# A fused attention and mixture-of-experts layer: the router's choice of groups by eight-largest and match-replace, and its steps placed on other tiles

## The chip, the cores and the metric

The kernel runs on one core of one Trainium2 chip. The number is the device time of one execution in microseconds (us). Durations inside come from one profiled execution.

## The reference

The layer takes x of shape (8, 512, 128), normalises it, puts it through 16-head attention with a residual and a second layer norm, adds that to x, normalises again and applies a mixture of 64 experts and one shared expert. What matters here is the router:

```python
scores = sigmoid(x @ router_w.T)                      # 64 experts
sfc = scores + e_bias
group_scores = top_k(sfc.reshape(T, 8, 8), 2)[0].sum(-1)   # 8 groups of 8
_, gidx = top_k(group_scores, 4)                      # best 4 groups
masked = where(expert in one of those groups, sfc, 0)
_, topk_idx = top_k(masked, 8)                        # best 8 experts
w = scores at topk_idx;  w = w / (w.sum(-1) + 1e-20) * 2.5
coef = w scattered to (T, 64)
h = silu(x @ Wg) * (x @ Wu) * coef ;  moe_out = h @ Wd (summed over experts)
```

Each of the eight sequences (512 tokens, 4 row tiles of 128) is one "block" of the expert part.

## The kernel before

The program has two parts. The first is attention over 64 pairs (sequence, two heads). The second is the expert part: eight blocks, numbered 0 to 7, of 33 tiles each: tile 0 is the shared expert, tiles 1 to 32 hold two experts each. All arithmetic on TensorE (PE) is done in split fp16, three matmuls for a product. Every engine has its own instruction stream, written out in order, and semaphores tie the streams together.

In iteration k of a block (`run_block`), PE issues `gate_up(k + 4)` (3 + 3 matmuls with 512 columns for a tile's gate and up products), then `down(k)` (3 matmuls that add tile k into the output). For one tile, ScalarE (ACT) applies silu (L693), VectorE (DVE) multiplies the up product with the coefficient row (L1006) and that with the gate (L1014, the tile is then `hid`), ACT makes the high half (L698), GpSimd (POOL) the low half (L535), and `down` takes both. Gate and up products lie in rings of three banks: `gate_up(t)` waits until `hid` of tile t-3 is there. So in iteration k PE waits for DVE's tile k + 1.

While block n runs, the routing of block n + 1 is computed in steps `route(m, r, k)`, k from 1 to 30. Four tables, `DVE_N`, `POOL_N`, `ACT_N` and `PE_N`, say behind which tile (on POOL, ahead of which tile) each engine does which step. Blocks 1 to 7 are routed this way; block 0 is routed during the last attention pairs, by the tables ending in `_0`. The steps are:

- 1 to 8: the second and third norm. POOL does the powers (L467, L469, steps 3 and 8), adds beta to x (L488, step 2), multiplies by gamma (L473) and adds x (L477); ACT scales rows (L610 in steps 4 and 5, L617 in 9 and 10). Step 7 on DVE reads what L477 wrote.
- 8 on PE (L1095): four transposes of the normed block, waiting for `xf_done` of ACT's step 10. ACT's 11 (L623) and DVE's 12 (L864) split the result, PE's 11 (12 matmuls with 64 columns) makes the logits.
- 14: ACT's sigmoid (L626), which reloads its function table before and after, and POOL's bias (L483).
- 16 to 19 on DVE: the two largest of each group and their sum, `gsum`. 20 to 22: the best four groups, by comparing all pairs of groups (L898 to L909). 23: the mask (L913). 24 and 25: the eight best experts (L918, L922). 26 to 28: normalised coefficients; L935 ends step 28 and raises `coef`.
- 27 on PE (L1110): four transposes of the coefficients. PE waits for `coef` in front of the `down` that comes before them. ACT's 30 (L630) copies them out, SyncE writes them to HBM and reads them back as rows broadcast over 64 partitions, two per tile, for L1006.

At a block's end, ACT copies the sum of the block before (L703, behind tile 3), PE turns it (L1251) and DVE adds it (L1019). `down` of the new block's tile 0 waits for that copy.

```python
                    if k == 27 and not last:
                        pe.wait_ge(coef, n + 2)
                    down(n, r, k)
```

`DVE_TAIL`, `PE_TAIL` and their like carry the last attention pieces in block 0 and are not changed. The functions and their callers:

Of the kernel before, what the change touches and what calls it, by code (L numbers as in the profile page):

```python
# [18 lines left out]
P = 128  # L19
# [11 lines left out]
QT = S // P  # L31
# [17 lines left out]
ROUTE_0 = 56  # L49


DVE_0 = {0: (1,), 1: (2,), 2: (3,), 9: (7,), 10: (8,), 15: (12,), 21: (16,), 22: (17,), 23: (18, 19), 24: (20, 21),
         25: (22, 23), 26: (24,), 27: (25,), 28: (26,), 29: (27,), 30: (28,)}
POOL_0 = {0: (1,), 2: (2,), 3: (3,), 7: (6,), 10: (8,), 20: (14,)}
ACT_0 = {5: (4,), 6: (5,), 12: (9,), 13: (10,), 15: (11,), 19: (14,), 31: (30,)}
PE_0 = {15: (8,), 19: (11,), 31: (27,)}


DVE_N = {1: (1,), 2: (2,), 3: (3,), 8: (7,), 9: (8,), 15: (12,), 19: (16,), 20: (17,), 21: (18, 19), 22: (20, 21),
         23: (22, 23), 24: (24,), 25: (25,), 26: (26,), 27: (27,), 28: (28,)}  # L60
POOL_N = {3: (3,), 5: (2,), 6: (6,), 9: (8,), 17: (14,)}
ACT_N = {5: (4,), 6: (5,), 11: (9,), 12: (10,), 14: (11,), 17: (14,), 30: (30,)}
PE_N = {11: (8,), 14: (11,), 27: (27,)}


PE_TAIL_UP = {2: ((64, 0),), 3: ((64, 1),), 4: ((64, 2), (64, 3))}
# [5 lines left out]
def layer(nc, x, Wq, bq, Wk, bk, Wv, bv, Wo, bo, gamma, beta, router_w, e_bias,  # L72
          Wg, Wu, Wd, SWg, SWu, SWd, out):
    with ExitStack() as ctx:  # L74
        def sem(name):
            return ctx.enter_context(nc.semaphore(name))
# [71 lines left out]
        ya = tiles4(take(S))  # L148
        bn, mean_var = tiles4(take(QT * 6)), tiles4(take(QT * 2))
        veps, rstd, total, share, nmean, shift = (take(QT) for _ in range(6))  # L150
        tri = take(G * G)
        assert top[0] <= xT_hi_at + dead
        top[0] = xT_lo_at
        xf = tiles4(take(S))
# [98 lines left out]
        route_step = sem("route_step")  # L253
        coef_out = sem("coef_out")
        coef_in = [sem(f"coef_in{i}") for i in range(4)]
        tri_done = sem("tri_done")
        g_ps = sem("g_ps")
        u_ps = sem("u_ps")
        silu_done = sem("silu_done")
# [170 lines left out]
        def _(pool):  # L430
# [23 lines left out]

            def route(m, r, k):

                if k == 1 and isinstance(m, int) and m == 0:

                    pool.wait_ge(scores_t, 8 * ROUTE_0)
                    pool.memset(tri, 1.0).then_inc(tri_done, 1)  # L460
                    pool.wait_ge(tri_done, 1)
                    pool.affine_select(out=tri.rearrange("p (g h) -> p g h", g=G), in_=tri.rearrange("p (g h) -> p g h", g=G),
                                       compare_op=ALU.is_gt, fill=0.0, base=0, pattern=[[1, G], [-1, G]],
                                       channel_multiplier=0).then_inc(tri_done, 1)
                if k in (3, 8):
                    pool.wait_ge(c_var, m * 2 + (1 if k == 3 else 2))
                    pool.tensor_tensor(rstd, veps, half_pow, ALU.pow).then_inc(rstd_pow, 1)  # L467
                    pool.wait_ge(rstd_pow, m * 2 + (1 if k == 3 else 2))
                    pool.tensor_tensor(shift, nmean, rstd, ALU.mult).then_inc(rstd_done, 1)  # L469
                if k == 6:  # L470

                    pool.wait_ge(scaled, m + 1)
                    pool.tensor_tensor(ya, ya, gamma_b.unsqueeze(1).broadcast_to([P, QT, D]), ALU.mult).then_inc(gained, 1)  # L473
                    wait(pool, out_sent, (m - 1) * 16)
# [250 lines left out]
        def _(dve):  # L725
# [95 lines left out]
            def route(m, r, k):  # L821
# [65 lines left out]
                if k == 19:  # L887
                    settled()
                    then(nc.vector.tensor_tensor(sec1, mid1, lo1, ALU.max))
                    own(nc.vector.tensor_tensor(gsum, hi1, sec1, ALU.add))  # L890

                mine = gsum.rearrange("p (t g) -> p t g", t=QT).unsqueeze(3).broadcast_to([P, QT, G, G])
                other = gsum.rearrange("p (t g) -> p t g", t=QT).unsqueeze(2).broadcast_to([P, QT, G, G])
                pairs3, pairs4 = (w.rearrange("p (t g h) -> p t g h", t=QT, g=G) for w in (work3, work4))
                taken, masked = (w.rearrange("p (t e) -> p t e", t=QT) for w in (work3, work4))
                if k == 20:
                    settled()
                    own(nc.vector.tensor_tensor(pairs4, other, mine, ALU.is_gt))  # L898
                    own(nc.vector.tensor_tensor(pairs3, other, mine, ALU.is_ge))
                if k == 21:  # L900
                    settled()
                    if isinstance(m, int) and m == 0:
                        dve.wait_ge(tri_done, 2)
                    then(nc.vector.tensor_tensor(taken, taken, all_tiles(tri), ALU.mult))
                    own(nc.vector.tensor_tensor(work3, work3, work4, ALU.max))
                if k == 22:
                    settled()
                    then(nc.vector.tensor_reduce(rank, work3.rearrange("p (n h) -> p n h", h=G), AX.X, ALU.add))
                    own(nc.vector.tensor_scalar(rank, rank, float(TOPG) - 0.5, None, ALU.is_lt))  # L909

                if k == 23:
                    settled()
# [129 lines left out]
        def _(pe):  # L1042
# [211 lines left out]
            def run_block(n, r, last):  # L1254
                for k in range(1, TILES if last else TILES + 1):
                    if not (last and k + 4 >= TILES):
                        gate_up(n, r, k + 4)
                    if k == 27 and not last:
                        pe.wait_ge(coef, n + 2)
                    down(n, r, k)  # L1260
                    if isinstance(n, int) and n == 0:
                        tail(run, PE_TAIL.get(k, ()))
                    if not last:
                        for part in PE_N.get(k, ()):
                            route(n + 1, 1 - r, part)
                transpose_sum(n, last)
# [3 lines left out]
            for k in range(5):  # L1270
# [54 lines left out]
```

## Time and profile before

| | |
|---|---|
| three runs, median (lowest to highest) | 1362.97 us (1359.21 to 1363.02) |
| the profiled execution | 1363.27 us, of which its span 1361.5 us |
| mean granted TensorE clock | 0.988 |
| PE busy, share of the span | 1295.1 us, 95% |
| VectorE busy | 1069.7 us, 79% |
| GpSimd busy | 1047.5 us, 77% |
| ScalarE busy | 870.9 us, 64% |
| expert part, end of the first block to the end | from about 868.8 to 1361.5 us |

Engine names in rows: PE is TensorE's matmuls, DVE is VectorE, ACT is ScalarE, POOL is GpSimd. L1044 is the helper through which nearly all matmuls pass. The timeline merges neighbouring instructions of one line (xN); the bracket is the idle time ahead of the row and what ended it.

### The profile page before, as it was taken

The page shows a single profiled execution, that of the slowest core. Times are in us where ns is not written, and L with a number is a line of the kernel's source. Part 1 is how long each engine was busy: PE and PEld are TensorE (multiplying, and loading weights), DVE is VectorE, ACT ScalarE, POOL GpSimd, SP SyncE. Part 2 cuts the span into 40 slices and gives each one's busy share as a digit, 9 for nine tenths or more (in the row PEclk, how much of TensorE's full clock was granted, in tenths as well). Part 3 has the DMA queues.
Part 4 walks back from the last instruction along what each step waited for, and adds up shares of the span by engine and source line. Part 5 has one row for each costly group of instructions (what it writes and reads, how often), then busy time and mean ns, then how long its engine had stood idle before and what let it go on. Part 6 is the DMA issues. An engine that isn't in the chain of part 4 may idle for free. (4 is left out here: it accounts for less than half of the span.)

```text
span 1361.5 us, 36458 instructions
## 1 busy us (share of the span) xinstructions
PE 1295.1 (95%) x12729; PEld 755.1 (55%) x12729; DVE 1069.7 (79%) x1898; ACT 870.9 (64%) x1588; POOL 1047.5 (77%) x1705
## 2 busy tenths in 40 slices
PE   3999999999999999999999899999999998999998
PEld 1576666666666666666666544444444343444443
DVE  6788888887777777777787878778877878787875
ACT  4677766666666666666666556566656575656554
POOL 2888888888888888888898866767667675767665
PEclk9899999999999999999999999999999999999999
DMA  7333333333333333333333043434343444434342
GB/s 188 78 83 78 82 78 73 86 76 81 74 78 79 82 75 79 78 81 75 81 81 79 6 128 117 135 117 144 117 132 123 121 134 121 131 116 148 100 157 91
DMA packets 126428, 135.60 MB, mean 100 GB/s; under 512 B 36112, under 2 KB 83536, under 8 KB 126288
## 3 DMA queue, kind: packets, MB, share of 16 engines
q1 hardware_dynamic: 126288, 133.71, 35.5%
q8 instruction: 91, 1.49, 0.5%
q14 instruction: 49, 0.40, 0.1%
HBM read 80.16 MB, written 3.15 MB: 61 GB/s over the span
## 5 line engine op out<-in xcount | busy, mean ns | idle before, releaser
L1044 PE MATMUL bank<-arena 128*128 128x65 f16 (+4 forms) x12344 | 1265.2, 264 | 51.3 <-DVE arena L1014 14.4
L1044 PEld LDWEIGHTS bank<-arena 128*128 128x128 f16 (+2 forms) x12344 | 709.8, 98 | 573.0 <-DVE arena L1014 37.8
L499 POOL TENSOR_TENSOR arena<-arena 128x256 f16<-128x256 f32 x1024 | 596.4, 614 | 102.5 <-ACT arena L654 101.6
L535 POOL TENSOR_TENSOR arena<-arena 128x256 f16<-128x256 f32 x528 | 344.6, 679 | 153.4 <-ACT arena L698 151.3
L950 DVE TENSOR_REDUCE arena<-bank 128x2 f32<-128x1024 f32 x256 | 311.9, 1219 | 54.2 <-PE bank L1044 50.3
L654 ACT ACTIVATE arena<-bank 128x512 f32<-128x512 f32 x512 | 276.6, 595 | 63.1 <-PE bank L1044 63.0
L698 ACT ACTIVATE arena<-arena 128x512 f16<-128x512 f32 x264 | 164.5, 623 | 156.3 <-DVE arena L1014 154.0
L1014 DVE TENSOR_TENSOR arena<-arena,bank 128x512 f32<-128x512 f32 x264 | 181.7, 688 | 61.5 <-ACT bank L693 38.0
L1006 DVE TENSOR_TENSOR arena<-arena,bank 128x512 f32<-128x512 f32 x256 | 174.9, 683 | 43.8 <-PE bank L1044 25.7
L693 ACT ACTIVATE bank<-bank 128x512 f32<-128x512 f32 x264 | 153.2, 581 | 46.7 <-PE bank L1044 46.3
L643 ACT ACTIVATE arena<-bank,arena 128x512 f16<-128x512 f32 x128 | 87.9, 687 | 143.1 <-PE bank L1044 143.1
L981 DVE SCALAR_TENSOR_TENSOR arena<-bank,arena 128x512 f16<-128x512 f32 x128 | 95.5, 746 | 17.6 <-ACT arena L643 14.6
L658 ACT ACTIVATE arena<-bank 2x1024 f16<-2x1024 f32 x64 | 64.9, 1014 | 22.0 <-PE bank L1044 21.8
L987 DVE TENSOR_TENSOR arena<-bank,arena 128x512 f16<-128x512 f32 x64 | 44.3, 691 | 40.9 <-ACT arena L675 40.9
L970 DVE TENSOR_TENSOR arena<-bank,arena 128x256 f32<-128x256 f32 x128 | 54.3, 424 | 4.4
L968 DVE RECIPROCAL arena<-bank 128x4 f32<-128x4 f32 x128 | 23.2, 182 | 35.5 <-PE bank L1044 35.4
L681 ACT ACTIVATE arena<-bank 128x512 f16<-128x512 f32 x64 | 37.7, 589 | 9.6 <-PE bank L1225 9.6
L959 DVE TENSOR_TENSOR arena<-bank,arena 128x512 f32 (+1 forms) x64 | 43.6, 681 | 0.0
L976 DVE TENSOR_TENSOR arena<-bank,arena 128x512 f16<-128x512 f32 x64 | 43.6, 681 | 0.0
L1225 PE MATMUL bank<-arena 128*128 128x128 f32 x256 | 39.3, 277 | 2.8 <-DVE arena L959 2.8
L1225 PEld LDWEIGHTS bank<-arena 128*128 128x128 f32 x256 | 32.4, 144 | 15.5 <-DVE arena L959 3.4
L675 ACT ACTIVATE arena<-bank 128x512 f16<-128x512 f32 x64 | 38.4, 600 | 2.4 <-PE bank L1044 0.9
(103 smaller groups left out, 415.9 us busy)
## 6 DMA issues: line engine op xcount, KB each, us to landing
arena<-coef_rows SPq DMA_DIRECT2D x512, 128.0 KB, 2.9
arena<-arena SPq DMA_DIRECT2D x384, 128.0 KB, 2.4
arena<-in_L_attn_x SPq DMA_DIRECT2D x9, 256.0 KB, 3.8
arena<-in_L_ffn_Wg SPq DMA_DIRECT2D x32, 64.0 KB, 2.2
arena<-in_L_ffn_Wu SPq DMA_DIRECT2D x32, 64.0 KB, 2.1
arena<-in_L_ffn_Wd SPq DMA_DIRECT2D x32, 64.0 KB, 2.1
out<-arena SPq DMA_DIRECT2D x8, 256.0 KB, 2.9
coef_rows<-arena SPq DMA_DIRECT2D x8, 128.0 KB, 2.2
```

What stands on the lines that cost most here:

```text
L499: last = pool.tensor_tensor(num_lo[:, u % 2, s, h, q], num[:, u % 2, s, h, q], num_hi[:, u % 2, s, h, q, 1], ALU.subtract)
L535: last = pool.tensor_tensor(hid_lo[:, r, at], hid[:, r, at], hid_hi[:, r, at], ALU.subtract)
L643: nc.scalar.activation(flat[:, (u + 3) % 2, (ZQH, ZKH)[which], :], proj_bank(t, which), ACT.Identity, bias=bias[:, n:n + 1]).then_inc(qk_h ...
L654: nc.scalar.activation(num[:, u % 2, s, h, :], ps_st[ST_BANK[2 * s + h]], ACT.Exp).then_inc(exp_done, 1)
L693: nc.scalar.activation(ps_gate[r % 3], ps_gate[r % 3], ACT.Silu).then_inc(silu_done, 1)
L698: nc.scalar.activation(hid_hi[:, r, :], hid[:, r, :], ACT.Copy).then_inc(hid_hi_done, 1)
L950: nc.vector.tensor_reduce(rmax[:, up % 2, q, :], max_bank(pair, q).rearrange("p (h k) -> p h k", h=2), AX.X, ALU.max).then_inc(max_done, 1)
L981: nc.vector.scalar_tensor_tensor(out=flat[:, (u + 3) % 2, (ZQL, ZKL)[s], :], in0=proj_bank(t, s), scalar=(bq8, bk_c)[s][:, n:n + 1], in1=f ...
L1006: nc.vector.tensor_tensor(prod[:, i % 2, :], coef_b[:, j % 4, :], ps_up[i % 3], ALU.mult).then_inc(prod_done, 1)
L1014: nc.vector.tensor_tensor(hid[:, i % 6, :], prod[:, i % 2, :], ps_gate[i % 3], ALU.mult).then_inc(hid_done, 1)
L1044: return nc.tensor.matmul(out_, lhsT, rhs, start=start, stop=stop, skip_group_check=True)
L1225: last = nc.tensor.transpose(ps_turn[:, k * P:(k + 1) * P], ctxn[:, u % 2, k, :], ident)
```

## The change

Three things change.

1. The best four groups are found as the experts are: `max` gives each row's eight group sums in falling order, a `memset` overwrites the last four of them with 3e38, `match_replace` puts -3e38 where one of the values that are left occurs, and a compare makes the mask. The pair comparisons, their triangle mask `tri` (POOL's step 1 of block 0) and step 22 go. The sums are over 4 row tiles, so `max` and `match_replace` are issued four times each, on 8 elements.
2. The tables place the steps on other tiles.
3. POOL's multiplication by gamma (L473) becomes step 5 of its own, ahead of tile 6; the addition of x (L477) stays step 6 and comes ahead of tile 7.

```diff
-DVE_N = {1: (1,), 2: (2,), 3: (3,), 8: (7,), 9: (8,), 15: (12,), 19: (16,), 20: (17,), 21: (18, 19), 22: (20, 21),
-         23: (22, 23), 24: (24,), 25: (25,), 26: (26,), 27: (27,), 28: (28,)}
-POOL_N = {3: (3,), 5: (2,), 6: (6,), 9: (8,), 17: (14,)}
-ACT_N = {5: (4,), 6: (5,), 11: (9,), 12: (10,), 14: (11,), 17: (14,), 30: (30,)}
-PE_N = {11: (8,), 14: (11,), 27: (27,)}
+DVE_N = {1: (1,), 2: (2,), 3: (3,), 9: (7,), 10: (8,), 15: (12,), 18: (16,), 19: (17,), 20: (18, 19), 21: (20,),
+         22: (21,), 23: (23,), 24: (24,), 25: (25,), 26: (26,), 27: (27, 28)}
+POOL_N = {3: (3,), 4: (2,), 6: (5,), 7: (6,), 10: (8,), 17: (14,)}
+ACT_N = {5: (4,), 6: (5,), 12: (9,), 13: (10,), 15: (11,), 17: (14,), 29: (30,)}
+PE_N = {10: (8,), 12: (11,), 24: (27,)}
...
                 if k == 19:
                     settled()
                     then(nc.vector.tensor_tensor(sec1, mid1, lo1, ALU.max))
-                    own(nc.vector.tensor_tensor(gsum, hi1, sec1, ALU.add))
+                    then(nc.vector.tensor_tensor(gsum, hi1, sec1, ALU.add))
...
+                groups, left = (w.rearrange("p (t g) -> p t g", t=QT) for w in (gsum, rank))
+                first = work2[:, 0:QT * G].rearrange("p (t g) -> p t g", t=QT)
                 if k == 20:
+                    for t in range(QT):
+                        own(nc.vector.max(first[:, t, :], groups[:, t, :]))
                     settled()
-                    own(nc.vector.tensor_tensor(pairs4, other, mine, ALU.is_gt))
-                    own(nc.vector.tensor_tensor(pairs3, other, mine, ALU.is_ge))
+                    own(nc.vector.memset(first[:, :, TOPG:], 3.0e38))
+                    settled()
                 if k == 21:
+                    for t in range(QT):
+                        own(nc.vector.match_replace(left[:, t, :], first[:, t, :], groups[:, t, :], -3.0e38))
                     settled()
-                    if isinstance(m, int) and m == 0:
-                        dve.wait_ge(tri_done, 2)
-                    then(nc.vector.tensor_tensor(taken, taken, all_tiles(tri), ALU.mult))
-                    own(nc.vector.tensor_tensor(work3, work3, work4, ALU.max))
-                if k == 22:
-                    settled()
-                    then(nc.vector.tensor_reduce(rank, work3.rearrange("p (n h) -> p n h", h=G), AX.X, ALU.add))
-                    own(nc.vector.tensor_scalar(rank, rank, float(TOPG) - 0.5, None, ALU.is_lt))
+                    own(nc.vector.tensor_scalar(rank, rank, -2.0e38, None, ALU.is_lt))
...
-                    if k == 27 and not last:
+                    if k == 24 and not last:
                         pe.wait_ge(coef, n + 2)
                     down(n, r, k)
```

The tables of block 0 change less: on DVE, behind the same slots, step 20 alone and then 21 and 23; on POOL `tri` goes, and the new steps 5 and 6 stand side by side as before.

**PE, a block with routing.** These are the matmuls of block 0's stream from the end of the attention pieces on; 9 matmuls with 512 columns are one iteration, L1095 (after: L1083) the norm's transposes, 128x64 the logits, L1110 (after: L1098) the coefficients' transposes, L1251 (after: L1239) the turned sum. Before:

```order
L1044 MATMUL bank<-arena 128x512 x54
L1095 MATMUL bank<-arena 128x128 x4
L1044 MATMUL bank<-arena 128x512 x27
L1044 MATMUL bank<-arena 128x64 x12
L1044 MATMUL bank<-arena 128x512 x117
L1110 MATMUL bank<-arena 64x128 x4
L1044 MATMUL bank<-arena 128x512 x54
L1251 MATMUL bank<-arena 128x128 x4
```

After:

```order
L1032 MATMUL bank<-arena 128x512 x45
L1083 MATMUL bank<-arena 128x128 x4
L1032 MATMUL bank<-arena 128x512 x18
L1032 MATMUL bank<-arena 128x64 x12
L1032 MATMUL bank<-arena 128x512 x108
L1098 MATMUL bank<-arena 64x128 x4
L1032 MATMUL bank<-arena 128x512 x81
L1239 MATMUL bank<-arena 128x128 x4
```

The norm's transposes moved up by one iteration, the logits by two, the coefficients' transposes by three.

**DVE, steps 20 to 24.** L1006 and L1014 (after: L994 and L1002) are the two multiplications of a tile; REGISTER_ALU rows prepare waits. Before, tiles 22 and 23:

```order
L1014 TENSOR_TENSOR arena<-arena,bank 128x512
L831 REGISTER_ALU
L898 TENSOR_TENSOR arena<-arena 128x256
L899 TENSOR_TENSOR arena<-arena 128x256
L831 REGISTER_ALU
L904 TENSOR_TENSOR arena<-arena 128x256
L831 REGISTER_ALU
L905 TENSOR_TENSOR arena<-arena 128x256
L1002 REGISTER_ALU
L1006 TENSOR_TENSOR arena<-arena,bank 128x512
L1014 TENSOR_TENSOR arena<-arena,bank 128x512
```

After, tiles 21 and 22:

```order
L1002 TENSOR_TENSOR arena<-arena,bank 128x512
L889 MAX arena<-arena 128x8 x4
L823 REGISTER_ALU
L891 MEMSET arena 128x4x4
L823 REGISTER_ALU
L990 REGISTER_ALU
L994 TENSOR_TENSOR arena<-arena,bank 128x512
L1002 TENSOR_TENSOR arena<-arena,bank 128x512
L895 MATCH_REPLACE arena<-arena 128x8 x4
L823 REGISTER_ALU
L897 TENSOR_SCALAR arena<-arena 128x32
L990 REGISTER_ALU
```

Four instructions on 256 elements (and two more behind the next tile) became ten on at most 32, spread over two tiles, one tile earlier.

## Rows read from the trace of the kernel before

Blocks are counted from 0. Iteration 12 of block 3 starts at 1036.38 us.

**Rows 1.** PE timeline, block 3: start us, us, engine, line, tiles, count [idle before].

```profile
1036.38 19.94 PE L1044 MATMUL bank<-arena 128*128 128x512 f16 x102
...
1057.44 2.12 PE L1044 MATMUL bank<-arena 128*128 128x512 f16 x9 [1.13 <-DVE arena L1014]
...
1071.37 11.17 PE L1044 MATMUL bank<-arena 128*128 128x512 f16 x51
...
1083.48 0.81 PE L1044 MATMUL bank<-arena 128*128 128x512 f16 x3 [0.93 <-ACT arena L703]
...
1084.12 0.60 PE L1251 MATMUL bank<-arena 128*128 128x128 f32 x4
```

**Rows 2.** PE timeline, last block: one stretch of 29 iterations without a wait.

```profile
1298.39 56.66 PE L1044 MATMUL bank<-arena 128*128 128x512 f16 x261
```

**Rows 3.** DVE timeline, block 3, tiles 18 to 28 with the routing of block 4.

```profile
1045.07 0.69 DVE L1014 TENSOR_TENSOR arena<-arena,bank 128x512 f32<-128x512 f32 x1 [2.62 <-ACT bank L693]
...
1053.99 0.42 DVE L898 TENSOR_TENSOR arena<-arena 128x256 f32<-128x256 f32 x1
...
1055.93 0.67 DVE L1006 TENSOR_TENSOR arena<-arena,bank 128x512 f32<-128x512 f32 x1
...
1057.30 0.41 DVE L908 TENSOR_REDUCE arena<-arena 128x32 f32<-128x256 f32 x1
...
1057.97 0.43 DVE L913 TENSOR_TENSOR arena<-arena 128x256 f32<-128x256 f32 x1
...
1059.97 0.60 DVE L918 MAX8 arena<-arena 128x8 f32<-128x64 f32 x4
...
1060.78 0.69 DVE L1006 TENSOR_TENSOR arena<-arena,bank 128x512 f32<-128x512 f32 x1 [0.21 <-DVE arena L918]
...
1062.16 0.08 DVE L922 MATCH_VALUE_LOAD arena<-arena 128x8 f32 x1
...
1062.36 0.08 DVE L922 MATCH_VALUE_LOAD arena<-arena 128x8 f32 x1
...
1068.84 0.42 DVE L935 TENSOR_TENSOR arena<-arena 128x256 f32<-128x256 f32 x1
```

**Rows 4.** ACT timeline, block 3, around the sigmoid.

```profile
1041.04 1.28 ACT L626 ACT_TABLE_LOAD   x1
...
1042.76 0.38 ACT L626 ACTIVATE arena<-bank 128x256 f32<-128x256 f32 x1 [0.43 <-PE bank L1044]
...
1044.45 0.58 ACT L693 ACTIVATE bank<-bank 128x512 f32<-128x512 f32 x1
```

**Rows 5.** DVE timeline, block 4's first tile with a coefficient.

```profile
1078.18 0.69 DVE L1006 TENSOR_TENSOR arena<-arena,bank 128x512 f32<-128x512 f32 x1 [1.80 <-DMA arena<-coef_rows]
```

**Rows 6.** PE timeline, six block periods: first and last of seven sums.

```profile
868.76 0.91 PE L1251 MATMUL bank<-arena 128*128 128x128 f32 x4
...
1297.95 0.60 PE L1251 MATMUL bank<-arena 128*128 128x128 f32 x4
```

**Rows 7.** PE timeline, blocks 4 to 5: a boundary with a longer wait.

```profile
1155.65 1.44 PE L1044 MATMUL bank<-arena 128*128 128x512 f16 x3 [2.11 <-ACT arena L703]
...
1156.88 1.06 PE L1251 MATMUL bank<-arena 128*128 128x128 f32 x4
...
1157.74 11.82 PE L1044 MATMUL bank<-arena 128*128 128x512 f16 x51
```

**Rows 8.** Windows: length, PE PEld DVE ACT POOL busy (count), PEclk, DMA, GB/s.

```profile
1157.00:1159.00 2.00, 2.00 (x8) 1.11 (x7) 0.99 (x6) 0.56 (x1) 0.00 (x0) 0.50 0.37 131
```

**Rows 9.** PE timeline, block 4: its sixth tile, and the norm's transposes.

```profile
1096.59 10.53 PE L1044 MATMUL bank<-arena 128*128 128x512 f16 x48 [0.86 <-POOL arena L535]
...
1106.96 0.60 PE L1095 MATMUL bank<-arena 128*128 128x128 f32 x4
```

**Rows 10.** ACT timeline, block 4: the second half of the norm's scaling.

```profile
1102.82 0.86 ACT L617 ACTIVATE arena<-arena 128x128 f32<-128x128 f32 x2
```

**Rows 11.** POOL timeline, attention part, after `tri` was made (686.7 to 687.5 us).

```profile
689.93 2.32 POOL L499 TENSOR_TENSOR arena<-arena 128x256 f16<-128x256 f32 x4 [0.16 <-ACT arena L654]
```

More of the change, by code:

```diff
@@ L49 @@
 ROUTE_0 = 56
-DVE_0 = {0: (1,), 1: (2,), 2: (3,), 9: (7,), 10: (8,), 15: (12,), 21: (16,), 22: (17,), 23: (18, 19), 24: (20, 21),
-         25: (22, 23), 26: (24,), 27: (25,), 28: (26,), 29: (27,), 30: (28,)}
-POOL_0 = {0: (1,), 2: (2,), 3: (3,), 7: (6,), 10: (8,), 20: (14,)}
+DVE_0 = {0: (1,), 1: (2,), 2: (3,), 9: (7,), 10: (8,), 15: (12,), 21: (16,), 22: (17,), 23: (18, 19), 24: (20,),
+         25: (21, 23), 26: (24,), 27: (25,), 28: (26,), 29: (27,), 30: (28,)}
+POOL_0 = {2: (2,), 3: (3,), 7: (5, 6), 10: (8,), 20: (14,)}
 ACT_0 = {5: (4,), 6: (5,), 12: (9,), 13: (10,), 15: (11,), 19: (14,), 31: (30,)}
 PE_0 = {15: (8,), 19: (11,), 31: (27,)}
-DVE_N = {1: (1,), 2: (2,), 3: (3,), 8: (7,), 9: (8,), 15: (12,), 19: (16,), 20: (17,), 21: (18, 19), 22: (20, 21),
-         23: (22, 23), 24: (24,), 25: (25,), 26: (26,), 27: (27,), 28: (28,)}
-POOL_N = {3: (3,), 5: (2,), 6: (6,), 9: (8,), 17: (14,)}
-ACT_N = {5: (4,), 6: (5,), 11: (9,), 12: (10,), 14: (11,), 17: (14,), 30: (30,)}
-PE_N = {11: (8,), 14: (11,), 27: (27,)}
+DVE_N = {1: (1,), 2: (2,), 3: (3,), 9: (7,), 10: (8,), 15: (12,), 18: (16,), 19: (17,), 20: (18, 19), 21: (20,),
[3 more added lines that the diff above has]
+PE_N = {10: (8,), 12: (11,), 24: (27,)}
 PE_TAIL_UP = {2: ((64, 0),), 3: ((64, 1),), 4: ((64, 2), (64, 3))}
@@ L150, in layer @@
         veps, rstd, total, share, nmean, shift = (take(QT) for _ in range(6))
-        tri = take(G * G)
         assert top[0] <= xT_hi_at + dead
@@ L255, in layer @@
         coef_in = [sem(f"coef_in{i}") for i in range(4)]
-        tri_done = sem("tri_done")
         g_ps = sem("g_ps")
@@ L455, in route @@
             def route(m, r, k):
[L457 to L464, printed above, removed]
                 if k in (3, 8):
@@ L469, in route @@
                     pool.tensor_tensor(shift, nmean, rstd, ALU.mult).then_inc(rstd_done, 1)
-                if k == 6:
+                if k == 5:
                     pool.wait_ge(scaled, m + 1)
                     pool.tensor_tensor(ya, ya, gamma_b.unsqueeze(1).broadcast_to([P, QT, D]), ALU.mult).then_inc(gained, 1)
+                if k == 6:
                     wait(pool, out_sent, (m - 1) * 16)
@@ L889, in route @@
                     then(nc.vector.tensor_tensor(sec1, mid1, lo1, ALU.max))
-                    own(nc.vector.tensor_tensor(gsum, hi1, sec1, ALU.add))
-                mine = gsum.rearrange("p (t g) -> p t g", t=QT).unsqueeze(3).broadcast_to([P, QT, G, G])
-                other = gsum.rearrange("p (t g) -> p t g", t=QT).unsqueeze(2).broadcast_to([P, QT, G, G])
-                pairs3, pairs4 = (w.rearrange("p (t g h) -> p t g h", t=QT, g=G) for w in (work3, work4))
+                    then(nc.vector.tensor_tensor(gsum, hi1, sec1, ALU.add))
                 taken, masked = (w.rearrange("p (t e) -> p t e", t=QT) for w in (work3, work4))
+                groups, left = (w.rearrange("p (t g) -> p t g", t=QT) for w in (gsum, rank))
+                first = work2[:, 0:QT * G].rearrange("p (t g) -> p t g", t=QT)
                 if k == 20:
+                    for t in range(QT):
+                        own(nc.vector.max(first[:, t, :], groups[:, t, :]))
                     settled()
-                    own(nc.vector.tensor_tensor(pairs4, other, mine, ALU.is_gt))
-                    own(nc.vector.tensor_tensor(pairs3, other, mine, ALU.is_ge))
+                    own(nc.vector.memset(first[:, :, TOPG:], 3.0e38))
+                    settled()
                 if k == 21:
+                    for t in range(QT):
+                        own(nc.vector.match_replace(left[:, t, :], first[:, t, :], groups[:, t, :], -3.0e38))
                     settled()
-                    if isinstance(m, int) and m == 0:
-                        dve.wait_ge(tri_done, 2)
-                    then(nc.vector.tensor_tensor(taken, taken, all_tiles(tri), ALU.mult))
-                    own(nc.vector.tensor_tensor(work3, work3, work4, ALU.max))
-                if k == 22:
-                    settled()
-                    then(nc.vector.tensor_reduce(rank, work3.rearrange("p (n h) -> p n h", h=G), AX.X, ALU.add))
-                    own(nc.vector.tensor_scalar(rank, rank, float(TOPG) - 0.5, None, ALU.is_lt))
+                    own(nc.vector.tensor_scalar(rank, rank, -2.0e38, None, ALU.is_lt))
                 if k == 23:
@@ L1300 @@
 ROUTE_COUNT = {1: 1, 2: QT, 3: QT + 1, 7: QT, 8: QT + 1, 16: 2, 17: 4, 18: 3, 19: 2,
-               20: 2, 21: 2, 22: 2, 23: 1, 24: QT, 25: QT, 26: 2, 27: 3, 28: 0}
+               20: QT + 1, 21: QT + 1, 23: 1, 24: QT, 25: QT, 26: 2, 27: 3, 28: 0}
 ROUTE_AT = {k: sum(c for j, c in ROUTE_COUNT.items() if j < k) for k in ROUTE_COUNT}
```

## The prediction

> **What bounds the kernel now.** I read first the timeline of PE over the expert part. Without a wait PE needs 56.66 us for 261 matmuls, 29 iterations, 1.95 us each [rows 2]. That is the floor, so only what makes PE wait, or slows its clock, counts. A routed block costs 33 x 1.95 = 64.4 us, three sets of transposes at 0.44 (1298.39 - 1297.95 [rows 2, 6]), and the logits' 0.4 (the stretch of x102 lasts 19.94, ten iterations 19.5 [rows 1]): 66.1 us. The six periods between the first and last sum of [rows 6] take (1297.95 - 868.76)/6 = 71.5. So 5.4 us of each block are waits and low clock.
>
> Then I looked at where. There are three places. (a) Near iteration 22 PE waits for DVE's `hid`, first 1.13 us [rows 1], then in smaller pieces, about 3 in all. DVE has no idle time there: from tile 18's L1014 at 1045.07 to the end of L935 at 1069.26 it runs for 24.19 us [rows 3], because a tile costs it only 1.37 (L1006 at 1055.93 to L908 at 1057.30), less than PE's 1.95, but routing steps lie between. The lag that PE forgives is large: `hid` of a tile may be about 3 us late. (b) At the boundary `down` of tile 0 waits for L703: 0.93 us [rows 1], 2.11 in another block [rows 7]. What is late is the coefficient rows: DVE waits 1.80 for them at the first tile [rows 5], and L703 stands behind that tile's successors on ACT. (c) In iteration 6 `down` waits 0.86 for POOL [rows 9].
>
> A wait has a second price. After the 2.11 us wait the granted clock is 0.50, the 1.2 GHz level [rows 8], and the same work takes longer than after the wait of 0.93: 1.44 against 0.81, 1.06 against 0.60, 11.82 against 11.17 [rows 7, 1], together 1.7 us. After the 1.13 and 0.93 waits nothing of it is seen.
>
> **The DVE steps.** Steps 20 to 22 take 1055.93 - 1053.99 = 1.94 and 1057.97 - 1057.30 = 0.67, together 2.61 us [rows 3]. The new ones aren't in the trace. Nearest rows: four `max` on 64 elements take 0.60, and 0.81 until the next tile starts; a value load and its match-replace follow each other every 0.20 (1062.16 to 1062.36) [rows 3]. On 8 elements I take 0.07 for each `max` and 0.14 for each pair, since narrower rows take less, plus some 0.2 to 0.25 each for the memset and the compare with the waits around them: 0.63 + 0.77 = 1.4. From above, at the 64-wide price: 0.81 + 0.25 and 0.80 + 0.45 = 2.3; from below 1.0. The saving is 1.2 us a block (0.3 to 1.6). Two further `settled` (step 19, and between 27 and 28) cost about 0.15.
>
> The Trainium skill (VectorE: DVE Perf Modes, the section on the TRN2 errata) speaks against this edit: an fp32 two-input operation takes (N + 151)/0.96 ns, so small ones pay nearly the whole fixed part each time, 166 ns for 8 elements. By that alone steps 20 and 21 would cost about 2.0 us, the saving would be 0.6, and the sum below would end 4 us higher. The pitch of the `max` and match-replace rows is shorter than the durations that this rule gives, so the trace does not bear it out for a run of such instructions without a wait between them.
>
> **The new order.** The important move is PE's. `pe.wait_ge(coef)` stood in iteration 27 and now stands in iteration 24, ahead of `down(24)`, while DVE raises `coef` behind tile 27 instead of 28. In a PE stream that does not wait, `gate_up(31)` has been issued by iteration 27, DVE is long past tile 28, and no wait for `coef` shows in [rows 1]. In iteration 24 it has only just issued `gate_up(28)`. Working it out in block 3:
>
> - PE: iteration 12 starts at 1036.38 before [rows 1], and by the terms under POOL below at nearly the same time after. Twelve iterations, the logits, and the 1.3 of a `gate_up`: 1036.4 + 23.4 + 0.4 + 1.3 = 1061.5, and some 0.15 for `hid` of tile 25, 1061.65. (The waits of (a) are gone up to there: steps 16 on start a tile earlier and 20 to 22 are shorter, so the lag of DVE passes 3 us only at tile 25.)
> - ACT: the sigmoid now waits for nothing. Before, it waited 0.43 for the logits, and ACT came to its table load (1041.04) late as well, since it had been held by the wait for the transposes. Table load, sigmoid and second load still take 1.28 + 0.4 + 1.28 ahead of tile 18's silu [rows 4]. I get 0.9 us earlier (0.43 + 0.45), so tile 18's L1014 at 1044.2.
> - DVE: from there without idle time, as before: 24.19, less one tile (1.37), less 1.2, plus 0.15: 21.75. `coef` comes at 1065.95.
>
> PE waits 1065.95 - 1061.65 = 4.3 us. Behind the wait stand `down(24)`, the transposes and `gate_up(29)`, so DVE runs dry too. Bounds: with 0.3 us more of a gain on ACT and the cheapest new steps 3.6; without any ACT gain and with the dearest 6.1.
>
> After it the clock. A wait of 2.11 was followed by the low level, waits of 1.13 and less were not, so one of 4.3 should be; I take the 1.7 us of above. Bounds: 0.9, if half of the low stretch falls into the wait, 2.6, if it lasts half as long again.
>
> **What the boundary gives back.** Relative to iteration 28 the coefficients leave about 4 us earlier. The 1.80 that they were late [rows 5] is covered, L703 runs when `down(32)` is done, and both the 0.93 and the 2.11 with its low clock go. I take zero for the boundary.
>
> **POOL.** L477 comes one L535 pair (1.3 us) later, so `down(6)` no longer waits [rows 9]; `down(7)` may for 0.2. But the norm is a chain: L477, step 7, step 8, L467, ACT's steps 9 and 10, PE's transposes. It now ends some 1.1 us later, while the transposes stand one iteration (1.95) earlier and the 0.86 that held PE up ahead of them is mostly gone. Before, ACT finished at 1102.82 + 0.86 = 1103.68 and the transposes began at 1106.96, 3.3 us later [rows 9, 10]. 3.3 - 1.1 - 1.95 - 0.8 = -0.6: PE waits 0.6 for `xf_done`. Bounds 0 to 1.2. Logits earlier by two iterations: ACT's step 11 stands at tile 15, its input is there, and the split is ready about 0.4 us before PE wants it: no wait.
>
> **Attention part.** Without `tri` POOL has two short operations less; 2.4 us later it idled 0.16 anyway [rows 11], so nothing is won. DVE's saving there is followed by waits on PE and ACT. I take 0, plus or minus 1.
>
> **The sum.** A block after: 66.1 + 0.2 (POOL) + 0.6 (norm) + 0.15 + 4.3 (`coef`) + 1.7 (clock) = 73.05, against 71.5: +1.55, six times +9.1 (from the unrounded mean). Block 0 with the routing of block 1 has the same new wait and loses a boundary wait of 2 us: +1. Total +10: 1363.3 + 10.1 = 1373.4 us. The profiled execution lies 0.3 above the median, so the same number stands against the runs.
>
> **Rivals.**
> 1. As worked out, 1373.4 (1367 to 1381 by the bounds): 0.57.
> 2. The new wait is there, but the clock stays at 2.4 GHz or the low stretch falls into the wait: seven times 1.7 less, 1361.5, no change. Against it: [rows 7, 8]. 0.12.
> 3. Faster. If DVE is much less behind at tile 27, the boundary's gain decides. The floor of 66.1 with 0.8 for POOL and norm leaves 4.6 for `coef` and clock before the block is as long as now; a wait of 1.5 without loss of clock gives 68.4, 3.1 less a block, 1342. It needs DVE 2.8 us earlier than I find. For it: with no lag at all the wait would be about 1. Against: the unbroken 24 us of DVE [rows 3]. 0.16.
> 4. Much slower: new steps at the dearest, ACT without its gain, and the longer low clock, 6.1 + 2.6 in place of 6.0: 2.7 a block more, about 1392. 0.05.
> 5. The new wait is real but costs only what (a) and (b) cost now, because DVE, not PE, sets the block: 1360 to 1366. 0.05.
> 6. The new steps cost the 2.3 us of the 64-wide rows, 0.9 more: `coef` and PE come later by that in seven blocks, 1373.4 + 6.3 = 1379.7. 0.05. This is what a fixed cost per instruction would do here; the rule of the Trainium skill named above (VectorE: DVE Perf Modes, TRN2 errata) is of that kind.
>
> **How the numbers follow.** A difference of 0.3% (4 us) is about what can be told. Slower: the first case but for 0.02 that falls short, the fourth and the sixth: 0.65. Same: the second, most of the fifth, those 0.02: 0.18. Faster: the third and the rest: 0.17. Range: up to 1382 it leaves out the fourth case; down to 1361 it takes in the second, and leaves out the third.
>
> **What would show it.** PE's timeline has one wait of 4 to 5 us for DVE (the coefficient product, L923 in the new file) ahead of three matmuls and the four transposes, in each of seven blocks, with a granted clock of 0.5 behind it; no wait for L703's counterpart; DVE idle behind the transposes; a wait of about 0.6 at the norm's transposes; none for POOL above 0.3. The four `max` on 8 elements take near 0.37. I am wrong if the `coef` wait is under 3 us, or if the clock stays high after it.

## The result, and the profile after

The changed kernel takes 1388.93 us (median of 4 runs, 1387.83 to 1389.89) against 1361.47 us (median of 4) for the kernel before on the same chip: ratio 1.021, 95% interval [1.0196, 1.0224]. It is slower, as forecast, but by 27 us and not by 10, and outside the range of 1361 to 1382. The profiled execution has a span of 1388.0 us.

PE's timeline in block 3 after (start us, us, engine, line, tiles, count, [idle before]), which answers to [rows 1]:

```profile
1023.24 19.64 PE L1032 MATMUL bank<-arena 128*128 128x512 f16 x90
1043.68 0.66 PE L1083 MATMUL bank<-arena 128*128 128x128 f32 x4 [0.79 <-ACT arena L609]
1044.17 27.78 PE L1032 MATMUL bank<-arena 128*128 128x512 f16 x135
1076.64 1.46 PE L1032 MATMUL bank<-arena 128*128 128x512 f16 x3 [4.69 <-DVE arena L923]
1077.90 1.06 PE L1098 MATMUL bank<-arena 128*64 128x128 f32 x4
1078.75 18.21 PE L1032 MATMUL bank<-arena 128*128 128x512 f16 x81
1096.80 0.60 PE L1239 MATMUL bank<-arena 128*128 128x128 f32 x4
```

The forecast wait is the fourth row: PE idles 4.69 us for DVE's L923 (the step that raises `coef`) ahead of `down(24)`, and the next row is the four transposes. The second row is the wait for `xf_done`, 0.79. The three matmuls behind the long wait take 1.46 us, the transposes 1.06, where [rows 1] has 0.81 and 0.60: the low clock. The stretch before the sum shows no wait for L695 (L703 before), and there is none for POOL in iteration 6.

Two rows each from other places on PE: the periods' first and last sum, which answer to [rows 6], and a wait for `hid` and one at a boundary, which answer to [rows 1, 7]:

```profile
870.64 0.60 PE L1239 MATMUL bank<-arena 128*128 128x128 f32 x4
...
1140.65 5.66 PE L1032 MATMUL bank<-arena 128*128 128x512 f16 x24 [0.45 <-DVE arena L1002]
...
1173.02 0.81 PE L1032 MATMUL bank<-arena 128*128 128x512 f16 x3 [2.20 <-ACT arena L695]
...
1324.42 0.60 PE L1239 MATMUL bank<-arena 128*128 128x128 f32 x4
```

Six periods take (1324.42 - 870.64)/6 = 75.6 us, against 71.5 before. At the boundary behind block 4, PE still waits 2.20 us for L695. I had put that at zero.

The granted clock behind a wait for `coef`, by windows (us, PE, PEld, DVE, ACT, POOL busy, PEclk, DMA share, GB/s), which answers to [rows 8]:

```profile
999.00:1001.00 2.00, 1.17 (x3) 0.46 (x4) 1.91 (x3) 0.00 (x0) 1.30 (x2) 0.50 0.36 94
1001.00:1003.00 2.00, 2.00 (x8) 1.14 (x7) 0.15 (x1) 0.00 (x0) 0.00 (x0) 0.50 0.49 120
1003.00:1005.00 2.00, 2.00 (x6) 0.71 (x5) 0.17 (x1) 1.54 (x3) 0.35 (x1) 0.55 0.03 11
1005.00:1007.00 2.00, 2.00 (x11) 0.88 (x9) 1.42 (x3) 0.91 (x3) 0.95 (x2) 1.00 0.32 74
```

The wait ends at 999.83. The clock stands at 0.50, the 1.2 GHz level, from then to beyond 1003, and is back at 1.00 in the last row.

DVE in block 3, which answers to [rows 3], with two rows of block 3's start:

```profile
1013.51 0.69 DVE L1002 TENSOR_TENSOR arena<-arena,bank 128x512 f32<-128x512 f32 x1 [0.19 <-DVE arena L998]
1016.86 0.69 DVE L994 TENSOR_TENSOR arena<-arena,bank 128x512 f32<-128x512 f32 x1 [2.67 <-PE bank L1032]
...
1053.99 0.69 DVE L1002 TENSOR_TENSOR arena<-arena,bank 128x512 f32<-128x512 f32 x1 [1.46 <-ACT bank L685]
...
1061.86 0.36 DVE L889 MAX8 arena<-arena 128x8 f32<-128x8 f32 x4
1062.30 0.07 DVE L891 MEMSET arena<- 128x16 f32 x1
1062.56 0.69 DVE L994 TENSOR_TENSOR arena<-arena,bank 128x512 f32<-128x512 f32 x1 [0.19 <-DVE arena L891]
...
1063.94 0.08 DVE L895 MATCH_VALUE_LOAD arena<-arena 128x8 f32 x1
...
1064.60 0.18 DVE L897 TENSOR_SCALAR arena<-arena 128x32 f32<-128x32 f32 x1
1064.77 0.69 DVE L994 TENSOR_TENSOR arena<-arena,bank 128x512 f32<-128x512 f32 x1
...
1066.15 0.42 DVE L901 TENSOR_TENSOR arena<-arena 128x256 f32<-128x256 f32 x1
...
1075.68 0.91 DVE L923 TENSOR_TENSOR arena<-arena 128x256 f32<-128x256 f32 x1
1076.51 0.67 DVE L994 TENSOR_TENSOR arena<-arena,bank 128x512 f32<-128x512 f32 x1
```

The first two rows are tile 0 and tile 1 of block 3. Between them lie 2.67 us without an instruction, where the same place in block 4 has 0.47; the profile puts them down to a PE instruction. The new steps cost 1062.56 - 1061.86 = 0.70 and 1064.77 - 1063.94 = 0.83 us. From tile 18's product (1053.99) to the end of L923 (1075.68 + 0.91 = 1076.59) DVE runs for 22.6 us, in blocks 2, 4 and 6 for 22.95. Below, "DVE's chain" is this stretch.

### The profile page after: what moved, and what is told of

Read it like the earlier page. It is cut to its first block and busy times, and to the rows that moved or that the text cites. A ratio compares the mean times of both kernels' runs of the same rounds, so it can differ in the third digit from the quotient of the medians.

```text
span 1388.0 us, 36513 instructions
## 1 busy us (share of the span) xinstructions
PE 1303.7 (94%) x12729; PEld 758.8 (55%) x12729; DVE 1070.5 (77%) x1962; ACT 872.5 (63%) x1588; POOL 1044.8 (75%) x1703
## 5 line engine op out<-in xcount | busy, mean ns | idle before, releaser
L994 DVE TENSOR_TENSOR arena<-arena,bank 128x512 f32<-128x512 f32 x256 | 175.4, 685 | 85.8 <-PE bank L1032 71.7
L1002 DVE TENSOR_TENSOR arena<-arena,bank 128x512 f32<-128x512 f32 x264 | 181.8, 689 | 45.1 <-ACT bank L685 20.0
L650 ACT ACTIVATE arena<-bank 2x1024 f16<-2x1024 f32 x64 | 64.9, 1014 | 21.1 <-PE bank L1032 21.0
L1213 PEld LDWEIGHTS bank<-arena 128*128 128x128 f32 x256 | 32.5, 144 | 15.6 <-DVE arena L947 3.5
```

The costliest lines, as they stand in the source:

```text
L994: nc.vector.tensor_tensor(prod[:, i % 2, :], coef_b[:, j % 4, :], ps_up[i % 3], ALU.mult).then_inc(prod_done, 1)
L1002: nc.vector.tensor_tensor(hid[:, i % 6, :], prod[:, i % 2, :], ps_gate[i % 3], ALU.mult).then_inc(hid_done, 1)
L1213: last = nc.tensor.transpose(ps_turn[:, k * P:(k + 1) * P], ctxn[:, u % 2, k, :], ident)
```

## The experiments

Each run has the kernel before beside it on the same chip, and the ratio is to that: 1360.9 us for runs 1 to 4, 1362.2 for runs 5 to 8, 1360.5 for runs 9 to 11. Line numbers shift by a few between kernels: L994 and L1002 are a tile's two products, L923 raises `coef`, L695 copies the sum.

**1. The coefficients' transposes back in iteration 27.**

```diff
-PE_N = {10: (8,), 12: (11,), 24: (27,)}
+PE_N = {10: (8,), 12: (11,), 27: (27,)}
-ACT_N = {... 29: (30,)}
+ACT_N = {... 30: (30,)}
-                    if k == 24 and not last:
+                    if k == 27 and not last:
                         pe.wait_ge(coef, n + 2)
```

> The changed kernel, but PE's step 27 and its wait for coef stand in iteration 27 again, and ACT's step 30 behind tile 30; all else as changed. Theory A (the early wait for coef, with the low clock behind it, is what costs): PE's wait of 4.7 us for DVE and the 2.3 us of low clock go in each of seven blocks, and about 2.5 us of short waits for hid come back: 4.5 x 7 = 31 us less than the changed kernel's 1389, about 1357, that is 0 to 1% under the kernel before. Theory B (the other moves, the norm's transposes and the ten small instructions, cost the time): 1380 or more.

1356.88 us, ratio to before 0.997 [0.9958, 0.9983]. Three numbers in the changed kernel, moved back, take 32 us off it; theory A had 1357. PE's timeline, around iteration 27 of block 3 and at two boundaries:

```profile
1007.71 0.81 PE L1032 MATMUL bank<-arena 128*128 128x512 f16 x3 [2.20 <-ACT arena L695]
...
1063.56 2.12 PE L1032 MATMUL bank<-arena 128*128 128x512 f16 x9 [0.95 <-DVE arena L1002]
1065.51 0.60 PE L1098 MATMUL bank<-arena 128*64 128x128 f32 x4
...
1077.84 0.81 PE L1032 MATMUL bank<-arena 128*128 128x512 f16 x3 [0.72 <-ACT arena L695]
```

In place of one wait of 4.7 there are short ones for `hid`, the last of them 0.95, and the boundary waits of the kernel before are back or longer (0.72 behind block 3, where the changed kernel has none, and 2.20 behind block 2, where it has 1.81). Everything else in the change together is worth 4 us of gain.

**2. The new choice of groups alone, in the kernel before.**

```diff
-... 22: (20, 21), 23: (22, 23), ...
+... 22: (20,), 23: (21, 23), ...
```

with steps 19 to 21 as in the change, and `tri` taken out.

> The kernel before with the new choice of groups alone: step 20 behind tile 22, steps 21 and 23 behind tile 23, every other step where it was, tri gone. Theory A (small instructions cost what the trace of the changed kernel shows, 0.70 and 0.83 us for the two steps against 2.61): DVE is 1 us less behind from tile 23 on, PE's short waits for hid shrink by about 1 us a block: about 1354, 0.5% faster. Theory B (ten small instructions each pay a full fixed part): same or slower, 1361 to 1366. Theory C (the saving is real but hidden by the boundary): 1361.

1359.08 us, ratio 0.9988 [0.9978, 0.9997]: not the 7 us of theory A, and not a loss as in B. Nor does the boundary hide a saving, as in C: its waits in the six periods add up to 7.2 us, against 6.6 before. DVE's timeline in block 3:

```profile
1043.15 0.69 DVE L1000 TENSOR_TENSOR arena<-arena,bank 128x512 f32<-128x512 f32 x1 [2.62 <-ACT bank L683]
...
1055.24 0.90 DVE L899 TENSOR_TENSOR arena<-arena 128x256 f32<-128x256 f32 x1
1056.69 0.69 DVE L992 TENSOR_TENSOR arena<-arena,bank 128x512 f32<-128x512 f32 x1 [0.54 <-DVE arena L899]
...
1066.94 0.42 DVE L921 TENSOR_TENSOR arena<-arena 128x256 f32<-128x256 f32 x1
```

From tile 18's product to the end of the step that raises `coef` it is 1066.94 + 0.42 - 1043.15 = 24.21 us, against 24.19 before [rows 3]; in blocks 2, 4 and 6 it is 23.85. So most of the microsecond saved in steps 20 to 22 is gone, or all of it. The mask's product now takes 0.90 where L913 took 0.43, and 0.54 idle follow: 1056.69 - 1055.24 = 1.45 us to the next tile's product, in place of 0.62 (in the trace of before that product starts at 1058.59, L913 at 1057.97). So the short steps are real and their saving is lost by the step behind them. On GpSimd an operation starts 0.05 us ahead of the mask's product, and in the changed kernel one starts 0.04 us ahead of L923, which takes 0.91:

```profile
1055.19 1.48 POOL L525 TENSOR_TENSOR arena<-arena 128x256 f16<-128x256 f32 x2 [0.79 <-ACT arena L688]
```

```profile
1075.64 1.48 POOL L527 TENSOR_TENSOR arena<-arena 128x256 f16<-128x256 f32 x2 [0.74 <-ACT arena L690]
```

The same holds for L905 before (0.78, beside a GpSimd pair from 1054.81 on). In blocks 3 and 4 of the three kernels, products of this shape with no GpSimd operation beside them take 0.42 or 0.43 (L898, L899 and L935 before, L901 and L915 after, L921 here), and a GpSimd pair with none of them beside it takes 1.30. So the long products go with a GpSimd operation that starts just ahead. That the one delays the other is argued; no run moves either.

**3. Matmuls ahead of the wait, to keep PE busy.**

```diff
                     if k == 24 and not last:
+                        pe.wait_ge(sigm, n + 2)
+                        for _ in range(18):
+                            mm(ps8[7], w_hi[:, k, 2, :], fT_hi[r], True, True)
                         pe.wait_ge(coef, n + 2)
```

> The changed kernel with 18 matmuls of 512 columns put ahead of the wait for coef in iteration 24; they write a PSUM bank that nobody reads. The wait lasts as long in time, but PE is busy for 3.9 of its 4.7 us. Theory A (the low clock behind the wait costs 2.3 us a block): no stretch at the 1.2 GHz level behind it, and 7 x 2.3 = 16 us less, about 1373. Theory B (the granted clock follows something else, or costs nothing since PE would wait later anyway): 1386 to 1390.

1374.57 us, ratio 1.0104 [1.0087, 1.0121], 14 us under the changed kernel, by adding work. PE in block 3, then a window behind a wait:

```profile
1069.92 0.82 PE L1032 MATMUL bank<-arena 128*128 128x512 f16 x3 [0.81 <-DVE arena L923]
1070.57 0.60 PE L1098 MATMUL bank<-arena 128*64 128x128 f32 x4
1071.01 17.64 PE L1032 MATMUL bank<-arena 128*128 128x512 f16 x81
1088.49 0.60 PE L1239 MATMUL bank<-arena 128*128 128x128 f32 x4
```

```profile
996.00:998.00 2.00, 2.00 (x12) 0.93 (x11) 0.64 (x2) 1.14 (x3) 0.00 (x0) 1.00 0.37 111
```

The idle time is 0.81, the transposes take 0.60, the clock is 1.00. From the end of the wait to the next sum it is 1088.49 - 1069.92 = 18.6 us; in the changed kernel 1096.80 - 1076.64 = 20.2, and 21.1 in another block (924.48 to 945.62). The mean over the four blocks without a boundary wait is 21.0. So the low clock costs 21.0 - 18.6 = 2.4 us a block, not my 1.7. The filler itself costs nothing: the wait ends 32.5 us after the first matmul behind the norm's transposes in both kernels (here that matmul starts at 1037.44, in the changed kernel at 1044.17).

**4. The norm's transposes one iteration later.**

```diff
-PE_N = {10: (8,), 12: (11,), 24: (27,)}
+PE_N = {11: (8,), 13: (11,), 24: (27,)}
```

> The changed kernel with PE's norm transposes behind iteration 11 and the logits behind 13, in place of 10 and 12. Theory A: the 0.8 us wait for xf_done goes in six blocks, but the logits come later against ACT's sigmoid (up to 0.4), and coef with them: 2 to 5 us less than the changed kernel, about 1385. Theory B (the wait costs nothing since the wait for coef takes it up, DVE being bound to ACT and not to PE): 1389, with the coef wait 0.8 us longer.

1381.70 us, ratio 1.0159 [1.0142, 1.0175], 7 us under the changed kernel, somewhat more than theory A's 2 to 5. The six periods are 74.5 us, in place of 75.6: 0.95 is the norm's wait, and the waits for `hid` ahead of `coef` are 0.4 shorter in block 3.

```profile
1039.71 0.60 PE L1083 MATMUL bank<-arena 128*128 128x128 f32 x4
...
1070.34 1.46 PE L1032 MATMUL bank<-arena 128*128 128x512 f16 x3 [4.69 <-DVE arena L923]
```

The transposes have no wait, and the wait for `coef` is as long as before, 4.69. Theory B, that it would grow by what the other lost, falls. I read it so: DVE's chain starts at the sigmoid, and that follows PE.

**5. The coefficients' transposes in iteration 26.** As experiment 1, with 26 for 27, and ACT's step 30 left at 29.

> The changed kernel with PE's step 27 and its wait for coef in iteration 26 in place of 24; ACT's step 30 stays behind tile 29. Theory A (PE must come to the wait just when DVE has raised coef, which in the run with iteration 27 was about 1.5 us ahead of that iteration's start): no wait of over 0.5 us and no low clock behind it, the four transposes lie in time that PE waited for hid anyway, and the coefficients reach DVE in time at every boundary without a loop's jump: 6 us less than with iteration 27, about 1351, 0.7% under the kernel before. Theory B (any place ahead of 27 makes PE wait for all of DVE's lag, 4.7 us less 1.95 an iteration): a wait near 1 us, 1360.

1350.61 us, ratio 0.9924 [0.9902, 0.9945].

```profile
1056.82 0.82 PE L1032 MATMUL bank<-arena 128*128 128x512 f16 x3 [0.22 <-DVE arena L923]
1057.48 0.60 PE L1098 MATMUL bank<-arena 128*64 128x128 f32 x4
...
1071.80 0.60 PE L1239 MATMUL bank<-arena 128*128 128x128 f32 x4
```

The wait is 0.22 us and the clock behind it is high (0.82 and 0.60). Three places for one wait: iteration 24 1389 (ratio 1.021), 26 1351 (0.992), 27 1357 (0.997). The rest is equal but for ACT's step 30, which is behind tile 30 in the last of them and behind 29 in the others.

**6. The early wait alone, in the kernel before.**

```diff
-PE_N = {11: (8,), 14: (11,), 27: (27,)}
+PE_N = {11: (8,), 14: (11,), 24: (27,)}
-                    if k == 27 and not last:
+                    if k == 24 and not last:
```

with ACT's step 30 at 29.

> The kernel before with one move alone: PE's step 27 and its wait for coef in iteration 24, ACT's step 30 behind tile 29; DVE raises coef behind tile 28 as before. Theory A: coef comes at about 1069.3 on the clock of the profile before, PE is at the wait at about 1063.5, so it waits near 6 us, then 2 us of low clock, and gets back the boundary's 1 to 3: 4 to 5 us more a block, about 1393. Theory B (the loss of the changed kernel needs its other moves too): under 1375.

1402.34 us, ratio 1.0303 [1.028, 1.0326]: 40 us from one move, 9 more than theory A had.

```profile
1027.11 0.81 PE L1044 MATMUL bank<-arena 128*128 128x512 f16 x3 [1.76 <-ACT arena L703]
...
1083.86 1.46 PE L1044 MATMUL bank<-arena 128*128 128x512 f16 x3 [5.54 <-DVE arena L935]
```

The wait is 5.54 us, near the 6 expected. The boundaries gave back less than the 1 to 3 us I had: their waits in the six periods add up to 4.0 us (1.76 here and 2.20 behind block 4) in place of 6.6, so 0.45 a block. A period is 77.4 us, 5.9 more than before and not 4 to 5.

**7. Norm and coefficients together:** `PE_N = {11: (8,), 13: (11,), 26: (27,)}`.

> The changed kernel with the norm's transposes behind iteration 11, the logits behind 13 and the coefficients' transposes and wait in 26. Theory A (the two waits add up, since each is in its own stretch of the block): a further 4 to 7 us under the run with iteration 26 alone, about 1346. Theory B (DVE is the bound from the sigmoid on, so an earlier norm is lost again at hid): 1350.

1342.36 us, ratio 0.986 [0.9838, 0.9881]. The two gains add up, 8 us here. What is left is in DVE's first tile of block 3 and, behind it, at PE's boundary between blocks 2 and 3:

```profile
996.36 0.69 DVE L994 TENSOR_TENSOR arena<-arena,bank 128x512 f32<-128x512 f32 x1 [3.11 <-PE bank L1032]
```

```profile
1001.66 0.81 PE L1032 MATMUL bank<-arena 128*128 128x512 f16 x3 [2.21 <-ACT arena L695]
```

**8. The same with DVE's loop over pairs of blocks written out.**

```diff
-            blocks(dve, run_block)
+            for n in range(B):
+                run_block(n, n % 2, n == B - 1)
```

> The run with the norm's transposes behind 11 and coef in 26, and DVE's loop over pairs of blocks written out, so that its stream has no jump back. Theory A (the boundary waits of 1.8 and 2.2 us for L695 that the changed kernel keeps behind blocks 2 and 4 come from DVE's jump back to the loop's start, 2.7 us without an instruction): both go, 4 us less, about 1342, and the clock stays high there. Theory B (they come from late coefficients or from the transfers of that moment): no change, 1346.

1329.63 us, ratio 0.977 [0.9748, 0.9791]: 13 us under run 7, three times theory A's 4. PE, two sums, then DVE:

```profile
930.18 0.60 PE L1240 MATMUL bank<-arena 128*128 128x128 f32 x4
...
996.79 0.60 PE L1240 MATMUL bank<-arena 128*128 128x128 f32 x4
```

```profile
1026.63 0.69 DVE L1002 TENSOR_TENSOR arena<-arena,bank 128x512 f32<-128x512 f32 x1 [1.11 <-ACT bank L685]
...
1047.39 0.91 DVE L923 TENSOR_TENSOR arena<-arena 128x256 f32<-128x256 f32 x1
```

A period is 66.6 us, 0.5 above the 66.1 that PE's work alone takes. No boundary wait is left. And DVE's chain is 1047.39 + 0.91 - 1026.63 = 21.7 us, 0.9 shorter than in the loop, with the same arithmetic: the tile's product behind the `memset` starts 0.11 us after it, in the loop 0.26. DVE's loop covers blocks 1 to 6, two to a turn, so it jumps back behind blocks 2 and 4; block 0 stands outside it. So the changed kernel itself can tell the two apart, in its block 0:

```profile
827.89 0.69 DVE L1002 TENSOR_TENSOR arena<-arena,bank 128x512 f32<-128x512 f32 x1 [1.46 <-ACT bank L685]
...
848.65 0.91 DVE L923 TENSOR_TENSOR arena<-arena 128x256 f32<-128x256 f32 x1
```

That is 848.65 + 0.91 - 827.89 = 21.7 us, ahead of any jump. What shortens the chain is to stand outside the loop, and not that the jump is gone. In the loop a wait on a count that depends on the block needs register instructions first, and they stand behind the wait ahead of them; that these are the difference is argued from the code.

**9. The changed kernel with DVE's loop written out.**

> The changed kernel with DVE's loop over pairs of blocks written out. In the runs before, DVE's chain from tile 18 to coef took 22.6 us in the loop and 21.7 written out, and the boundary wait behind blocks 2 and 4 went. Theory A (both are added to the early wait): the wait for coef falls from 4.7 to 3.8 us in seven blocks, two waits of 2 us go, the clock still falls: 1389 - 6.5 - 4.2 = 1378. Theory B (a shorter wait lets the clock stay high): 1365.

1376.11 us, ratio 1.0118 [1.01, 1.0135]; theory A had 1378.

```profile
1069.31 1.46 PE L1033 MATMUL bank<-arena 128*128 128x512 f16 x3 [4.48 <-DVE arena L923]
```

The total is A's, the split isn't: the wait for `coef` only falls to 4.48, since PE, no longer held up for `hid`, comes to it earlier too.

**10. The kernel before with DVE's loop written out.**

> The kernel before with DVE's loop written out and nothing else. Theory A: DVE's chain is near 0.9 us shorter, so the waits for hid shrink by 0.9 in seven blocks, and the boundary waits of 2.2 and 2.1 us with their low clock become near 0.9: 1361 - 6 - 5 = 1350. Theory B (the new choice of groups is needed to make use of it): 1358 to 1361.

1352.01 us, ratio 0.9942 [0.9923, 0.9961], near A's 1350.

```profile
1006.53 0.81 PE L1045 MATMUL bank<-arena 128*128 128x512 f16 x3 [1.14 <-ACT arena L703]
```

The boundary wait behind block 2 is 1.14 in place of 2.20, so here the jump was only half of it: DVE still waits for coefficient rows. Its chain is 23.5 us, 0.7 shorter and not 0.9.

**11. The changed kernel with DVE's loop shifted:** blocks 0, 1, 6 and 7 written out, two turns over the rest, one jump back, behind block 3.

> The changed kernel with DVE's loop shifted: blocks 0, 1, 6 and 7 are written out, the loop runs twice over blocks 2 and 3 and blocks 4 and 5, so that DVE jumps back once, behind block 3, in place of twice, behind 2 and 4. Theory A (the jump makes the wait): one wait of 2 us for L695's counterpart at the boundary behind block 3, none behind 2 and 4; 2 to 3 us less than the changed kernel, 1386. Theory B (block parity, transfers): waits stay behind 2 and 4, 1389.

1382.32 us, ratio 1.0159 [1.0141, 1.0178], 4 less than A had. The written-out blocks gain as in 9: DVE's chain is 21.66 us in blocks 1 and 6 and 22.6 in the four blocks of the loop.

```profile
1094.55 0.81 PE L1038 MATMUL bank<-arena 128*128 128x512 f16 x3 [1.60 <-ACT arena L695]
```

This is the only wait for L695 at a boundary between blocks, and it stands behind block 3. Behind 2 and 4 there is none. The wait moves with the jump, and theory B falls.

## Why the prediction was right in its direction and wrong in its size

**The main mechanism held.** "PE waits 1065.95 - 1061.65 = 4.3 us" is 4.7 in the trace. ACT's gain came too: tile 18's product is 7.9 us behind the start of iteration 12 (1053.99 less 1044.17 and one iteration), 8.7 before. Experiments 1, 5 and 6 show that this one place accounts for the loss: without it the changed kernel is 0.3 to 0.8% faster than before, and alone it costs 3.0%.

**The sum was mis-sized, in nearly every term, and upwards.** I had 73.05 us a block over a floor of 66.1, so 6.95 of waits and clock; measured are 75.6 and 9.5:

| term, us a block | forecast | measured | where it is read |
|---|---|---|---|
| wait for `coef` | 4.3 | 4.7 | 1076.64 |
| waits for `hid` ahead of it | 0.15 | 0.75 | 1076.64 - 1044.17 = 32.5, less 4.7, less 27.0 of work; 0.35 more in blocks 2, 4 and 6 |
| low clock | 1.7 | 2.4 | experiment 3 |
| boundary | 0 | 0.7 | 1.81 and 2.20 in two of six |
| wait for `xf_done` | 0.6 | 0.95 | 1043.68 - 1023.24 = 20.4, less 19.5 |
| POOL | 0.2 | 0 | no wait |

The differences add up to 2.5 us a block, 15 us in six. The rest is 0.9: up to the end of block 0, 1.9 us was lost (870.64 - 868.76) and not 1. Behind the last sum both kernels take 63.6.

**The step on DVE.** "24.19, less one tile (1.37), less 1.2, plus 0.15: 21.75" came out at 22.6. The new steps took 1.53, near the 1.4. What I left out are the last product, at 0.91 in place of 0.42, and, as I read it, more of the loop's register waits behind a step that ends in `settled` (0.19 at L994 in the rows above). Written out, the same chain takes 21.7. This made both the wait and the `hid` waits ahead of it longer.

**The step on the boundary is the one that failed as reasoning.** "I take zero for the boundary": I read the wait of DVE for coefficient rows [rows 5] as the cause of all boundary waits. In blocks 1, 3 and 5 that was so, and they went. Behind blocks 2 and 4 of the changed kernel it is DVE's jump to the start of its loop, as 9 and 11 show; before, it was half of the wait (run 10). The unequal waits in the trace before (0.93 against 2.11) were the sign of it, and I put both down to one cause. The step cost 0.7 us a block, 4 of the 15; the larger part of the miss is that of the other terms.

**The clock.** "I take the 1.7 us of above" was the loss after a wait of 2.1. After 4.7 it is 2.4, within the bounds I gave.

**The range.** Each bound that I gave was right for its term, but I let them offset each other. Most of the errors had the same sign, and some the same cause. And the waits for `hid` and the boundary had no bound at all; they are 1.3 of the 2.5 us. The time lies near rival 4 (1392, with a chance of 0.05), but not by its mechanism: its longer low clock came true (2.6, measured 2.4), while its dear new steps, the lost gain on ACT and so the wait of 6.1 us did not.

**The rule of the Trainium skill** (VectorE: DVE Perf Modes, the section on the TRN2 errata), a nearly full fixed part for each small operation, gave an estimate of 2.0 us for the two steps. Measured are 1.53: four `max` on 8 elements take 0.36 together. The rule doesn't hold here for a run of small instructions without a wait between them. Rival 6, which needed 2.3 us for the steps, is out. Rival 2 (the clock stays) and rival 3 (DVE less far behind) are refuted by the windows and by the 4.7 us wait. The norm and POOL terms were right in kind, and experiment 4 shows the norm's wait as a loss of its own.

Open is whether it is GpSimd that lengthens the mask's product in experiment 2 and L923 in the changed kernel, why the `hid` waits differ between odd and even blocks, and why the time lost to the low clock differs by 1.4 us between blocks (20.2 to 21.5 us from the wait to the sum).

## What to carry to other kernels

A wait on the engine that bounds the kernel belongs where the awaited engine has just finished, with its backlog counted, not where its last step stands in the table: iteration 24, 26 or 27 of 33 made 1389, 1351 or 1357 us. A step that is moved earlier on the waiting engine gains nothing if its input comes at the same time. Before taking one cause for a row of like waits, compare them from block to block: two sizes can be two causes, and a period of two pointed to the loop.

## What the runs showed of the hardware

- 18 useless matmuls ahead of a wait saved 14 us, because the granted clock behind it stayed at 2.4 GHz (run 3).
- At its jump to the start of a long loop body DVE has no instruction for 2.5 to 3.8 us (2.46 in run 11, 3.75 in run 4), where the boundaries without a jump in these two runs have 0.37 to 0.58. The profile names PE as the releaser, or none. By the Trainium skill (Runtime: NRT & Kernel Launch, the section on instruction fetch mechanics), a taken branch to a target outside the instructions held makes the engine fetch it before it goes on. The page gives no price. The stretch without an instruction agrees; no run shows the fetch itself.
- Outside its loop DVE's chain in a block's routing is 0.9 us of 22.6 shorter (block 0 of the changed kernel, blocks 1 and 6 of run 11), which I put down to waits computed in registers. Those and the jumps together are 13 us of 1342 (runs 7 and 8).
- Four `max` instructions on 8 elements take 0.36 us, on 64 elements 0.60.
- A product of 256 elements with both inputs in SBUF takes 0.42 us on DVE, and 0.78 to 0.91 where a GpSimd operation has just started (before, after, run 2); the cause is argued.
